# Adjacency: one-hots of two tiles in one DVE operation, alternating with single adds; relation nodes: two relations in each matmul

## The chip, the cores and the metric

The kernel runs on one core of one Trainium2 chip. The metric is the device time of one launch in microseconds (us), as the median of several runs. PE is the matmul engine (PEld its weight loads), DVE the vector engine, ACT the scalar engine, POOL is GpSimd, SP issues most DMAs. Each engine has a sequencer that issues its instructions in program order, waits for semaphores, and does register work in between; rows of a sequencer carry a q behind the engine's name (DVEq).

## The reference, cut to what matters

A stack of four graph layers on 3125 nodes with 48 features and 100000 edges. Two places of it matter here.

```python
# layers 1 and 2: 5 and 10 steps of sums over the edges of the same graph
m = jax.ops.segment_sum(w[:, None] * h[row], col, num_segments=n)
...
msg = f[src] * edge_weight[:, None]
agg = jax.ops.segment_sum(msg, dst, num_segments=n)
...
# layer 3: eight relations, two small layers for each node and relation
h1 = jax.nn.relu(jnp.einsum('ni,rij->nrj', inputs, weight1) + bias1)
h2 = jnp.einsum('nrj,rjo->nro', h1, weight2)
msg = h2[src, rel_type] * norm
agg = jax.ops.segment_sum(msg, dst, num_segments=inputs.shape[0])
return jax.nn.relu(agg + bias2)
```

The sums over edges of layers 1 and 2 are done as products with a dense matrix of the graph, which the stage `adjacency` builds once.

## The kernel before

Nodes lie in 25 blocks (NB) of 128. The edges have been sorted into 1488 tiles of 128 edges, each of one pair of blocks, and four tiles (G) make a group: 372 groups (NG). Stages follow each other with a barrier of all engines between them; the two that are changed are `adjacency` and `relation_nodes`.

**`adjacency`.** For each tile DVE compares a row 0 to 127 with the edge's source and destination numbers, which gives two one-hot matrices of 128 by 128: `turned[..., 2]` for the sources, `hd` for the destinations. PE turns both round (`turn`, for later gathers, stored as OHT) and multiplies them (`products`): once as they are, which counts edges, and once with ACT's widened copy `hs_wide` and its weighted copy `hd_weighted`. DVE then adds each tile's 256 columns to `acc`, at a place that depends on the tile's blocks (`add_up`). When a block of sources is finished, POOL stores its row of ADJ.

Every engine walks through its own list of stages, group by group, in `laps`: a stage with lag 2 works in turn n on group n - 2, six slots hold groups in flight, and a loop over registers covers six groups in a lap, after twelve groups written out. DVE's list (line 876) is: one-hots of the sources of group n (four operations, lines 841 to 843), `rows` for group n - 2, the first add, one-hots of the destinations of group n (four, line 848), and three more adds. `rows` loads four numbers from `row_at` into registers (TENSOR_LOAD, line 853); they hold the places of the four tiles in `acc`. An add waits for the one ahead of it (`s_acc`, line 869), as both may write the same place; the first add of a group also waits for the group's products (`s_sums`).

ACT's list in a turn: widen the sources, weight the destinations, copy the turned matrices of the group before. PE's list: turn, then products.

**`relation_nodes`.** x is turned round to `xT` (48 features by 3200 nodes). Then for each of the eight relations: seven matmuls of at most 512 nodes give the hidden layer (`hidden`, line 2105), ACT adds the bias and cuts at zero (line 2090), 25 matmuls of 128 nodes give h2 with 48 columns each (line 2116), and DVE copies them out of PSUM (line 2126). PE does the hidden layer of relation r + 1 ahead of the products of relation r. When all eight are there, one DMA stores H2 (line 2076), and the stage `relation_pass` gathers rows from it.

Of the kernel before, what the change touches and what calls it, by code (L numbers as in the profile page):

```python
# [18 lines left out]
ALU = mybir.AluOpType  # L19
# [700 lines left out]
def adjacency(nc, mem):  # L720
# [4 lines left out]
    with ExitStack() as ctx:  # L725
# [16 lines left out]
        with nc.Block() as block:  # L742
# [86 lines left out]
            def _(dve):  # L829
                v = nc.vector  # L830
                at = {}

                def column(b, j, at):
                    return rec[:, b, j, at - CW:at - CW + 1]

                def sources(n, b, lap):
                    dve.wait_ge(s_rec[b], 16 * lap + 16)
                    if past(lap, 1):
                        dve.wait_ge(s_sums, n - (SLOTS - 1))
                        dve.wait_ge(s_oht[b], 16 * lap)  # L840
                    for j in range(G):
                        last = v.tensor_scalar(turned[:, b, j, 2], mem["iota_bf"][:], column(b, j, SL), None,
                                               ALU.is_equal)
                    last.then_inc(s_hs, 1)

                def destinations(n, b, lap):
                    for j in range(G):
                        last = v.tensor_scalar(hd[:, b, j], mem["iota_bf"][:], column(b, j, DL), None, ALU.is_equal)
                    last.then_inc(s_hot, 1)

                def rows(n, b, lap):

# [8 lines left out]
                def add_up(j):  # L861

                    def stage(n, b, lap):
# [4 lines left out]
                        if j > 0 or past(n, 1):  # L868
# [119 lines left out]
def past(n, count):  # L988

    return not isinstance(n, int) or n >= count  # L990
# [1063 lines left out]

def relation_nodes(nc, mem, io):

    with ExitStack() as ctx:
        room = Room(nc, ctx, "q_")
        xT = room.sb("xT", [H, NB * P])
        h1T = room.sb("h1T", [H, 2, NB * P])  # L2060
        h2 = room.sb("h2", [P, NB, RELS * H])
        w1 = room.sb("w1", [H, RELS, H])
        w2 = room.sb("w2", [H, RELS, H])
        b1 = room.sb("b1", [H, 1])
        s_w, s_turned, s_copied, s_h1, s_h1c, s_h2, s_h2c, s_out = (
            room.sem(n) for n in ("s_w", "s_turned", "s_copied", "s_h1", "s_h1c", "s_h2", "s_h2c", "s_out"))
        banks = [room.ps(f"bank{b}", [P, 512]) for b in range(2)]
        h2p = [room.ps(f"h2p{b}", [P, 3, 512]) for b in range(2)]
        with nc.Block() as block:
            @block.sync  # L2070
            def _(sp):
                sp.dma_start(w1[:], io["L3_gnn_weight1"].rearrange("r i j -> i r j")).then_inc(s_w, 16)
                sp.dma_start(w2[:], io["L3_gnn_weight2"].rearrange("r i j -> i r j")).then_inc(s_w, 16)
                sp.dma_start(b1[:], io["L3_gnn_bias1"].rearrange("(p o) -> p o", o=1)).then_inc(s_w, 16)
                sp.wait_ge(s_h2c, RELS)
                sp.dma_start(mem["H2"].rearrange("(c p) w -> p c w", p=P), h2[:]).then_inc(s_out, 16)
                sp.wait_ge(s_out, 16)

            @block.scalar
            def _(act):  # L2080
                copy_turned(nc, act, xT, H, banks, s_turned, s_copied)
                act.wait_ge(s_w, 48)
                for r in range(RELS):
                    if r >= 2:
                        act.wait_ge(s_h2, r - 1)
                    for q in range(QUADS):
                        n = min(4, NB - 4 * q) * P
                        m = r * QUADS + q
                        act.wait_ge(s_h1, m + 1)
                        nc.scalar.activation(h1T[:, r % 2, 4 * q * P:4 * q * P + n], banks[m % 2][0:H, 0:n],  # L2090
                                             ACT.Relu, bias=b1[:, 0:1]).then_inc(s_h1c, 1)

            @block.tensor
            def _(pe):
                turn_nodes(nc, pe, mem["x"], H, banks, s_turned, s_copied, mem["ident"][:])
                pe.wait_ge(s_copied, QUADS)
                pe.wait_ge(s_w, 48)

                def hidden(r):
                    for q in range(QUADS):  # L2100
                        n = min(4, NB - 4 * q) * P
                        m = r * QUADS + q
                        if m >= 2:
                            pe.wait_ge(s_h1c, m - 1)
                        nc.tensor.matmul(banks[m % 2][0:H, 0:n], w1[:, r], xT[:, 4 * q * P:4 * q * P + n],
                                         start=True, stop=True).then_inc(s_h1, 1)

                hidden(0)
                for r in range(RELS):
                    if r + 1 < RELS:  # L2110
                        hidden(r + 1)
                    pe.wait_ge(s_h1c, (r + 1) * QUADS)
                    if r >= 2:
                        pe.wait_ge(s_h2c, r - 1)
                    for c in range(NB):
                        last = nc.tensor.matmul(h2p[r % 2][:, c // SPB, (c % SPB) * H:(c % SPB + 1) * H],
                                                h1T[:, r % 2, c * P:(c + 1) * P], w2[:, r], start=True, stop=True)
                    last.then_inc(s_h2, 1)

            @block.vector  # L2120
            def _(dve):
                for r in range(RELS):
                    dve.wait_ge(s_h2, r + 1)
                    for c in range(3):
                        n = min(SPB, NB - c * SPB)
                        last = nc.vector.tensor_copy(h2[:, c * SPB:c * SPB + n, r * H:(r + 1) * H],
                                                     h2p[r % 2][:, c, 0:n * H].rearrange("p (c w) -> p c w", w=H))
                    last.then_inc(s_h2c, 1)


def relation_pass(nc, mem):
# [160 lines left out]
```

## Time and profile before

| | us |
|---|---|
| median of 3 runs | 10251.57 |
| lowest and highest | 10250.43, 10257.3 |
| the profiled execution | 10251.39 |
| its span, first to last instruction | 10249.6 |

Over the span PE is busy 71%, DVE 59%, ACT 37%, POOL 46%. The page's chain of work that ended last is traced back only through the last stage, so it says nothing of the two stages here; they are read from windows and timelines. The profile's busy times count an instruction from its start to the end of its result, so two that follow each other closely overlap: the distance from start to start is what an operation costs in a row of independent ones. Idle time is given in brackets with what ended it; "issue" is time in which the engine waited for nothing that the profile shows.

### The profile page before, as it was taken

How to read it: one execution, taken by the hardware profiler on the slowest of the kernel's cores; microseconds unless marked ns; L12 is line 12 of the kernel's file. 1: busy time of each engine (PE TensorE's matmuls, PEld its weight loads, DVE VectorE, ACT ScalarE, POOL GpSimd, SP SyncE). 2: the span in 40 equal slices, each digit the busy share in tenths (PEclk: the TensorE clock that was granted, in tenths of full speed). 3: DMA queues.
4: the chain of work that ended last, by engine and by line, in shares of the span. 5: the costliest groups of instructions: out<-in, count | busy, mean ns of one | idle time of the engine just before them, and what ended most of it. 6: DMA issues, size and time to landing. Idle time of an engine off the chain costs nothing. (4 is left out here: it accounts for less than half of the span.)

```text
span 10249.6 us, 319174 instructions
## 1 busy us (share of the span) xinstructions
PE 7281.1 (71%) x106850; PEld 5832.8 (57%) x106851; DVE 6047.0 (59%) x19984; ACT 3752.5 (37%) x13000; POOL 4708.0 (46%) x6246
## 2 busy tenths in 40 slices
PE   2888856667657849976994997699488788832332
PEld 1555535555547749966993996699334344432332
DVE  6555558888867779977996998799510000011112
ACT  3222217777743326744772675477100000100000
POOL 0777760000016625533551553355275677256665
PEclk9999998887879979988996998899699999755555
DMA  8222215555439949956992995699488999311112
GB/s 324 60 63 61 62 46 175 183 181 182 132 106 312 310 135 259 262 139 178 262 263 58 260 263 154 165 262 262 138 320 316 351 364 364 130 34 18 18 18 18
DMA packets 1832085, 1846.79 MB, mean 180 GB/s; under 512 B 1450037, under 2 KB 1467989, under 8 KB 1786741
## 3 DMA queue, kind: packets, MB, share of 16 engines
q1 hardware_dynamic: 1717890, 1668.62, 53.0%
q0 software_dynamic: 112016, 153.10, 5.8%
q10 hardware_dynamic: 2016, 22.94, 0.6%
q8 instruction: 97, 1.59, 0.1%
q14 instruction: 66, 0.54, 0.0%
HBM read 1481.79 MB, written 360.62 MB: 180 GB/s over the span
## 5 line engine op out<-in xcount | busy, mean ns | idle before, releaser
L1639 POOL TENSOR_TENSOR s_rest<-s_msg 128x196 f32<-128x196 f32 x1488 | 762.5, 512 | 1912.5 <-ACT s_msg L1621 1861.1
L1231 PE MATMUL s_gotd<-m_table_d,s_hot 128*128 x17856 | 1364.6, 205 | 207.4 <-DMA s_hot<-OHT 195.2
L1621 ACT ACTIVATE s_msg<-s_gotd,s_es 128x49 f32<-128x49 f32 x5952 | 1304.5, 303 | 48.4
L1231 PE MATMUL s_gotq<-m_table_s,s_hot 128*128 x17856 | 1280.9, 185 | 11.3 <-issue 11.3
L1231 PEld LDWEIGHTS s_gotd<-m_table_d,s_hot 128*128 128x128 bf16 x17856 | 990.2, 96 | 293.2 <-DMA s_hot<-OHT 196.3
L1901 POOL DMA_INDIRECT REC<-m_sums x800 | 958.0, 1198 | 354.3 <-issue 347.3
L463 POOL DMA_INDIRECT REC<-rec,place x800 | 960.5, 1201 | 260.5 <-issue 225.8
L2164 POOL DMA_INDIRECT l_row<-H,l_rec x816 | 785.5, 963 | 616.0 <-DMA l_rec<-REC 310.8
L1672 DVE TENSOR_REDUCE s_tops<-s_mt 128x512 f32 (+1 forms) x1488 | 1013.7, 681 | 6.7 <-PE s_mt L1582 6.4
L1934 PE MATMUL p_acc<-p_row,p_feats 128*64 128x512 f32 (+1 forms) x4032 | 900.6, 570 | 160.7 <-DMA p_row<-ADJ 157.8
L1231 PEld LDWEIGHTS s_gotq<-m_table_s,s_hot 128*128 128x128 bf16 x17856 | 993.2, 97 | 7.4 <-issue 7.4
L1245 PE MATMUL l_sums<-l_msg,l_oh 128*128 128x49 f32 x1632 | 371.8, 380 | 824.2 <-issue 807.9
L871 DVE SCALAR_TENSOR_TENSOR a_acc<-a_acc,m_keep,a_sums 128x256 f32 x1488 | 713.2, 479 | 241.2 <-DVE a_acc L871 122.3
L1245 PEld LDWEIGHTS l_sums<-l_msg,l_oh 128*128 128x128 f32 x1632 | 377.2, 322 | 820.1 <-issue 819.9
L1581 PE MATMUL s_mt<-s_hot,m_apart 128*128 128x128 bf16 x5952 | 823.9, 219 | 6.1 <-issue 4.3
L1582 PE MATMUL s_mt<-m_ident_bf,s_raw 128*128 128x128 bf16 x5952 | 824.3, 219 | 1.2 <-issue 1.2
L1646 POOL TENSOR_TENSOR s_least<-s_rest 128x196 bf16<-128x196 f32 x1488 | 762.9, 513 | 116.7
L1934 PEld LDWEIGHTS p_acc<-p_row,p_feats 128*64 128x64 f32 x4032 | 386.1, 141 | 654.6 <-issue 431.1
L822 PE MATMUL a_sums<-a_hd_weighted,a_hs_wide 128*128 128x128 f32 x2976 | 685.3, 359 | 0.0
L1602 PE MATMUL s_sums<-s_msg,s_hot 128*128 128x49 bf16 x5952 | 619.7, 186 | 47.2 <-issue 39.5
L1602 PE MATMUL s_sums<-s_rest,s_hot 128*128 128x49 bf16 x5952 | 620.9, 186 | 0.0
L1602 PE MATMUL s_sums<-s_least,s_hot 128*128 128x49 bf16 x5952 | 619.1, 184 | 0.1
(423 smaller groups left out, 18556.8 us busy)
## 6 DMA issues: line engine op xcount, KB each, us to landing
s_hot<-OHT SPq DMA_DIRECT2D x1488, 384.0 KB
p_row<-ADJ SPq DMA_DIRECT2D x288, 1600.0 KB
s_rec<-REC SPq DMA_DIRECT2D x1488, 98.0 KB
OHT<-a_turned SPq DMA_DIRECT2D x372, 384.0 KB
g_hot<-OHT SPq DMA_DIRECT2D x372, 384.0 KB
ADJ<-a_acc POOLq DMA_DIRECT2D x25, 3200.0 KB
REC<-fill SPq DMA_DIRECT2D x124, 624.0 KB, 10.3
g_rec<-REC SPq DMA_DIRECT2D x372, 108.0 KB
```

Of the source, the lines that this page charges most:

```text
L463: nc.gpsimd.indirect_dma_start(out=mem["REC"], out_offset=bass.IndirectOffsetOnAxis(ap=place[:, b, j:j + 1], axis=0), in_=rec[:, b, j], in ...
L1231: last = nc.tensor.matmul(out, hot, table[k][:, bass.ds(at, w)], start=(k == 0), stop=(k == 2))
L1581: nc.tensor.matmul(mt[:, j], mem["apart"][:], hot[:, b, j, 1], start=True, stop=False)
L1582: last = nc.tensor.matmul(mt[:, j], upper(raw[:, b % KEPT, j:j + 1]).to_broadcast([P, P]), mem["ident_bf"][:], start=False, stop=True)
L1602: last = nc.tensor.matmul(sums[:, 0:SW], hot[:, b, j, 2], thirds[k], start=(j == 0 and k == 0), stop=(j == G - 1 and k == 2))
L1621: last = nc.scalar.activation(msg[:, b % KEPT, j], gotd[b % KEPT][:, j, SW:2 * SW], ACT.Copy, scale=es[:, b % 2, j:j + 1])
L1639: nc.gpsimd.tensor_tensor(rest[:, b % KEPT].rearrange("p g w -> p (g w)"), msg[:, b % KEPT].rearrange("p g w -> p (g w)"), upper(msg[:, b ...
L1646: nc.gpsimd.tensor_tensor(least[:, b % KEPT].rearrange("p g w -> p (g w)"), rest[:, b % KEPT].rearrange("p g w -> p (g w)"), upper(rest[:, ...
L1672: v.tensor_reduce(tops[:, bass.ds(n, 1)], mt[:].rearrange("p j e -> p (j e)"), X, ALU.max).then_inc(s_top, 1)
L1901: nc.gpsimd.indirect_dma_start(out=mem["REC2"], out_offset=bass.IndirectOffsetOnAxis(ap=places_of[b][:, t:t + 1], axis=0), in_=numbers_of[ ...
L1934: last = nc.tensor.matmul(acc[odd * SIDE:(odd + 1) * SIDE, q, 0:n * P].rearrange("w (c e) -> w c e", e=P), feats[:, s], source.rearrange(" ...
L2164: nc.gpsimd.indirect_dma_start(out=row[:, b, j], out_offset=None, in_=table, in_offset=bass.IndirectOffsetOnAxis(ap=rec[:, b, j, GIDX - NO ...
```

## The change

In `adjacency` one DVE operation (`hots`) makes the one-hots of two tiles, as a tensor_tensor from the f32 row `iota` and the f32 record numbers in place of a tensor_scalar from the bf16 row. The list of DVE's stages is written anew: `rows` comes first, and each of the four operations on pairs of tiles stands ahead of one add.

In `relation_nodes` two relations are put side by side: the weights of the hidden layer give 96 output rows in one matmul, and the second weights stand as a 96 by 96 matrix with two blocks on its diagonal, zero elsewhere (a POOL memset, then two DMAs into the blocks). The products go into six PSUM tiles of five nodes' blocks by 96 columns, with a semaphore for each, and H2 is stored in four pieces, one for each pair of relations.

```diff
-                def sources(n, b, lap):
-                    dve.wait_ge(s_rec[b], 16 * lap + 16)
...
-                    for j in range(G):
-                        last = v.tensor_scalar(turned[:, b, j, 2], mem["iota_bf"][:], column(b, j, SL), None,
-                                               ALU.is_equal)
-                    last.then_inc(s_hs, 1)
-
-                def destinations(n, b, lap):
-                    for j in range(G):
-                        last = v.tensor_scalar(hd[:, b, j], mem["iota_bf"][:], column(b, j, DL), None, ALU.is_equal)
-                    last.then_inc(s_hot, 1)
+                def hots(out, b, pair, at):
+                    tiles = slice(2 * pair, 2 * pair + 2)
+                    return v.tensor_tensor(out, mem["iota"][:].unsqueeze(1).to_broadcast([P, 2, P]),
+                                           rec[:, b, tiles, at - CW:at - CW + 1].to_broadcast([P, 2, P]), ALU.is_equal)
+
+                def sources(pair):
+
+                    def stage(n, b, lap):
+                        if pair == 0:
+                            dve.wait_ge(s_rec[b], 16 * lap + 16)
...
+                        last = hots(turned[:, b, 2 * pair:2 * pair + 2, 2], b, pair, SL)
+                        if pair == 1:
+                            last.then_inc(s_hs, 1)
+                    return stage
+
+                def destinations(pair):
+
+                    def stage(n, b, lap):
+                        last = hots(hd[:, b, 2 * pair:2 * pair + 2], b, pair, DL)
+                        if pair == 1:
+                            last.then_inc(s_hot, 1)
+                    return stage
...
-                laps(dve, [(sources, 0), (rows, 2), (add_up(0), 2), (destinations, 0), (add_up(1), 2),
-                               (add_up(2), 2), (add_up(3), 2)], SLOTS)
+                laps(dve, [(rows, 2), (sources(0), 0), (add_up(0), 2), (sources(1), 0), (add_up(1), 2),
+                           (destinations(0), 0), (add_up(2), 2), (destinations(1), 0), (add_up(3), 2)], SLOTS)
...
+    PAIR, FIVE = 2 * H, 5
+    TWOS, PARTS, BANKS = RELS // 2, NB // FIVE, 6
...
+                sp.wait_ge(s_zero, 1)
+                for k in range(2):
+                    sp.dma_start(w2[k * H:(k + 1) * H, :, k * H:(k + 1) * H],
+                                 io["L3_gnn_weight2"].rearrange("(t k) i j -> k i t j", k=2)[k]).then_inc(s_w, 16)
+                for t in range(TWOS):
+                    sp.wait_ge(s_h2c, (t + 1) * PARTS)
+                    sp.dma_start(mem["H2"].rearrange("(c p) w -> p c w", p=P)[:, :, t * PAIR:(t + 1) * PAIR],
+                                 h2[:, :, t * PAIR:(t + 1) * PAIR]).then_inc(s_out, 16)
...
+                        nc.tensor.matmul(banks[m % 2][0:PAIR, 0:n],
+                                         w1[:, 2 * t:2 * t + 2].rearrange("i r j -> i (r j)"),
+                                         xT[:, 4 * q * P:4 * q * P + n], start=True, stop=True).then_inc(s_h1, 1)
...
+                    for c in range(PARTS):
+                        k = t * PARTS + c
+                        if k >= BANKS:
+                            pe.wait_ge(s_h2c, k - BANKS + 1)
+                        for i in range(FIVE):
+                            node = c * FIVE + i
+                            last = nc.tensor.matmul(h2p[k % BANKS][:, i], h1T[:, t % 2, node * P:(node + 1) * P],
+                                                    w2[:, t], start=True, stop=True)
+                        last.then_inc(s_h2, 1)
```

Two places in the engines' order show what moves. The first is one turn of DVE in the adjacency stage before, between two groups of the loop; `a_turned` are the sources, `a_hd` the destinations, `a_acc` an add, ISA the wait ahead of it.

```order
L842 TENSOR_SCALAR a_turned<-m_iota_bf,a_rec 128x128 x4
L853 TENSOR_LOAD m_row_at
L866 REGISTER_ALU x2
L871 ISA
L871 SCALAR_TENSOR_TENSOR a_acc<-a_acc,m_keep,a_sums 128x2x128
L848 TENSOR_SCALAR a_hd<-m_iota_bf,a_rec 128x128 x4
L871 ISA
L871 SCALAR_TENSOR_TENSOR a_acc<-a_acc,m_keep,a_sums 128x2x128
L871 ISA
L871 SCALAR_TENSOR_TENSOR a_acc<-a_acc,m_keep,a_sums 128x2x128
L871 ISA
L871 SCALAR_TENSOR_TENSOR a_acc<-a_acc,m_keep,a_sums 128x2x128
```

The same turn of DVE after the change, from the load to the last add.

```order
L861 TENSOR_LOAD m_row_at
L835 TENSOR_TENSOR a_turned<-m_iota,a_rec 128x2x128
L874 REGISTER_ALU x2
L879 ISA
L879 SCALAR_TENSOR_TENSOR a_acc<-a_acc,m_keep,a_sums 128x2x128
L835 TENSOR_TENSOR a_turned<-m_iota,a_rec 128x2x128
L879 ISA
L879 SCALAR_TENSOR_TENSOR a_acc<-a_acc,m_keep,a_sums 128x2x128
L835 TENSOR_TENSOR a_hd<-m_iota,a_rec 128x256
L879 ISA
L879 SCALAR_TENSOR_TENSOR a_acc<-a_acc,m_keep,a_sums 128x2x128
L835 TENSOR_TENSOR a_hd<-m_iota,a_rec 128x256
```

The last add follows this piece. The one-hots have moved between the adds, the load has moved from behind the sources' one-hots to ahead of their first operation, and the destinations' last operation now stands just ahead of the last add.

The second place is PE in the relation nodes, first the last rows of the stage before; `q_h2p` are the products of the second layer, `q_bank` is the hidden layer.

```order
L2116 MATMUL q_h2p<-q_w,q_h1T 128x48 x25
L2105 MATMUL q_bank<-q_xT,q_w 48x512 x6
L2105 MATMUL q_bank<-q_xT,q_w 48x128
L2116 MATMUL q_h2p<-q_w,q_h1T 128x48 x25
L2105 MATMUL q_bank<-q_xT,q_w 48x512 x6
L2105 MATMUL q_bank<-q_xT,q_w 48x128
L2116 MATMUL q_h2p<-q_w,q_h1T 128x48 x50
```

The same last rows of PE in the stage after the change.

```order
L2141 MATMUL q_h2p<-q_w,q_h1T 128x96 x25
L2126 MATMUL q_bank<-q_xT,q_w 96x512 x6
L2126 MATMUL q_bank<-q_xT,q_w 96x128
L2141 MATMUL q_h2p<-q_w,q_h1T 128x96 x25
L2126 MATMUL q_bank<-q_xT,q_w 96x512 x6
L2126 MATMUL q_bank<-q_xT,q_w 96x128
L2141 MATMUL q_h2p<-q_w,q_h1T 128x96 x50
```

The sequence is the same, but there are four rounds in place of eight, with 96 output rows in the hidden layer and 96 columns in the second. On SP the one DMA of H2 at the stage's end has become four, each behind the copies of its pair of relations.

## Rows read from the trace of the kernel before

**Rows 1.** Windows, the two stages: length, busy us of each engine (instructions), clock, DMA, GB/s.

```profile
1536.00:2975.00 1439.00, 985.17 (x7440) 814.74 (x7440) 1181.60 (x4466) 1038.99 (x2233) 29.20 (x31) 0.82 0.49 164
8831.00:9023.20 192.20, 174.34 (x537) 106.98 (x537) 12.30 (x24) 38.27 (x63) 0.00 (x0) 0.52 0.08 27
```

**Rows 2.** Timeline of DVE, adjacency: start, duration, line, operation, count, [idle before it].

```profile
2013.27 0.48 DVE L871 SCALAR_TENSOR_TENSOR a_acc<-a_acc,m_keep,a_sums 128x256 f32 x1 [0.23 <-issue]
2013.67 0.74 DVE L848 TENSOR_SCALAR a_hd<-m_iota_bf,a_rec 128x128 bf16<-128x128 bf16 x4
2014.32 0.48 DVE L871 SCALAR_TENSOR_TENSOR a_acc<-a_acc,m_keep,a_sums 128x256 f32 x1
2014.96 0.48 DVE L871 SCALAR_TENSOR_TENSOR a_acc<-a_acc,m_keep,a_sums 128x256 f32 x1 [0.17 <-DVE a_acc L871]
2015.61 0.48 DVE L871 SCALAR_TENSOR_TENSOR a_acc<-a_acc,m_keep,a_sums 128x256 f32 x1 [0.17 <-DVE a_acc L871]
...
2016.91 0.48 DVE L871 SCALAR_TENSOR_TENSOR a_acc<-a_acc,m_keep,a_sums 128x256 f32 x1 [0.17 <-issue]
...
2021.19 0.48 DVE L871 SCALAR_TENSOR_TENSOR a_acc<-a_acc,m_keep,a_sums 128x256 f32 x1 [0.81 <-PE a_sums L822]
```

**Rows 3.** Line 853, DVE's sequencer: duration ns min/median/max, first and last start.

```profile
L853 DVEq FUSED_REGOPS  x1: 65/65/65, 2015.9 to 2015.9; - x1
...
L853 DVEq TENSOR_LOAD <-m_row_at x1: 982/982/982, 2019.6 to 2019.6; - x1
```

**Rows 4.** The same line in the last quarter of the stage, 101 loads.

```profile
L853 DVEq TENSOR_LOAD <-m_row_at x101: 340/343/972, 2595.2 to 2969.2; - x101
```

**Rows 5.** Windows, the relation nodes without their start and end.

```profile
8844.00:9006.00 162.00, 161.75 (x497) 102.16 (x497) 10.76 (x21) 30.86 (x51) 0.00 (x0) 0.50 0.00 0
```

**Rows 6.** Timeline of the relation nodes, from the last weight transfers to the next stage.

```profile
8832.29 0.46 SPq L2074 DMA_DIRECT2D q_b<-in_L_gnn_bias  x1
...
8836.58 7.32 PE L2105 MATMUL q_bank<-q_xT,q_w 48*48 48x512 f32 x14 [0.39 <-ACT q_xT L1081]
...
8876.73 10.90 PE L2116 MATMUL q_h2p<-q_w,q_h1T 48*128 48x48 f32 x50
...
8887.56 10.90 PE L2105 MATMUL q_bank<-q_xT,q_w 48*48 48x512 f32 x14
...
8898.39 10.90 PE L2116 MATMUL q_h2p<-q_w,q_h1T 48*128 48x48 f32 x50
...
9006.60 1.54 DVE L2126 COPY q_h<-q_h2p 128x480 f32<-128x480 f32 x3 [9.13 <-PE q_h2p L2116]
9008.17 0.40 SPq L2076 DMA_DIRECT2D H<-q_h  x1
...
9023.95 0.50 PEld L1238 LDWEIGHTS l_sums<-m_zeros,m_nothing 1*128 1x128 f32 x2 [17.55 <-issue]
```

**Rows 7.** Two lines with tensor_tensor on DVE: duration ns min/median/max, starts.

```profile
L565 DVE TENSOR_TENSOR ohb<-sblk,m_iota x100: 682/685/686, 265.1 to 1430.6; 125x512 bf16<-125x512 f32 x100
...
L1391 DVE TENSOR_TENSOR g_gated<-g_rec,g_scaled x372: 349/356/709, 3052.7 to 3662.5; 128x192 f32<-128x192 f32 x186
```

**Rows 8.** Timeline of DVE in an attention stage: a tensor_tensor and the operation behind it.

```profile
4005.61 0.35 DVE L1664 TENSOR_TENSOR s_prod<-s_key,s_gotq 128x196 f32<-128x196 f32 x1
4005.88 0.16 DVE L1684 TENSOR_TENSOR s_diff<-s_diff,m_cap 128x4 f32<-128x4 f32 x1
```

**Rows 9.** Timeline of ACT and of PE, adjacency.

```profile
2010.74 1.28 ACT L791 ACTIVATE a_hd_weighted<-a_hd,a_rec 128x128 f32<-128x128 bf16 x4 [0.68 <-DVE a_hd L848]
...
2024.68 0.31 PE L820 MATMUL a_sums<-a_hd,a_turned 128*128 128x128 bf16 x1
2024.79 0.74 PE L822 MATMUL a_sums<-a_hd_weighted,a_hs_wide 128*128 128x128 f32 x2
2025.32 0.31 PE L820 MATMUL a_sums<-a_hd,a_turned 128*128 128x128 bf16 x1
```

**Rows 10.** Line 1464 in an attention stage, at granted clock 0.50: f32 products with 96 columns.

```profile
L1464 PE MATMUL t_qk<-t_w,t_hT x24: 417/417/417, 4640.7 to 4645.6; 48*128 48x96 f32 x24
```

More of the change, by code:

```diff
@@ L2072, in _ @@
                 sp.dma_start(w1[:], io["L3_gnn_weight1"].rearrange("r i j -> i r j")).then_inc(s_w, 16)
[L2073 to L2077, printed above, removed]
+                for k in range(2):
+                    sp.dma_start(b1[k * H:(k + 1) * H], io["L3_gnn_bias1"].rearrange("(p o) -> p o", o=1)
+                                 ).then_inc(s_w, 16)
+                sp.wait_ge(s_zero, 1)
+                for k in range(2):
+                    sp.dma_start(w2[k * H:(k + 1) * H, :, k * H:(k + 1) * H],
[4 more added lines that the diff above has]
+                                 h2[:, :, t * PAIR:(t + 1) * PAIR]).then_inc(s_out, 16)
+                sp.wait_ge(s_out, 16 * TWOS)
+            @block.gpsimd
+            def _(pool):
+                nc.gpsimd.memset(w2[:], 0.0).then_inc(s_zero, 1)
             @block.scalar
@@ L2081, in _ @@
                 copy_turned(nc, act, xT, H, banks, s_turned, s_copied)
[L2082 to L2085, printed above, removed]
+                act.wait_ge(s_w, 80)
+                for t in range(TWOS):
+                    if t >= 2:
+                        act.wait_ge(s_h2, (t - 1) * PARTS)
                     for q in range(QUADS):
                         n = min(4, NB - 4 * q) * P
-                        m = r * QUADS + q
+                        m = t * QUADS + q
                         act.wait_ge(s_h1, m + 1)
-                        nc.scalar.activation(h1T[:, r % 2, 4 * q * P:4 * q * P + n], banks[m % 2][0:H, 0:n],
+                        nc.scalar.activation(h1T[:, t % 2, 4 * q * P:4 * q * P + n], banks[m % 2][0:PAIR, 0:n],
                                              ACT.Relu, bias=b1[:, 0:1]).then_inc(s_h1c, 1)
@@ L2096, in _, with hidden @@
                 pe.wait_ge(s_copied, QUADS)
-                pe.wait_ge(s_w, 48)
-                def hidden(r):
+                pe.wait_ge(s_w, 80)
+                def hidden(t):
                     for q in range(QUADS):
                         n = min(4, NB - 4 * q) * P
-                        m = r * QUADS + q
+                        m = t * QUADS + q
                         if m >= 2:
                             pe.wait_ge(s_h1c, m - 1)
-                        nc.tensor.matmul(banks[m % 2][0:H, 0:n], w1[:, r], xT[:, 4 * q * P:4 * q * P + n],
-                                         start=True, stop=True).then_inc(s_h1, 1)
+                        nc.tensor.matmul(banks[m % 2][0:PAIR, 0:n],
+                                         w1[:, 2 * t:2 * t + 2].rearrange("i r j -> i (r j)"),
+                                         xT[:, 4 * q * P:4 * q * P + n], start=True, stop=True).then_inc(s_h1, 1)
@@ L2108, in _ @@
                 hidden(0)
[L2109 to L2118, printed above, removed]
+                for t in range(TWOS):
+                    if t + 1 < TWOS:
+                        hidden(t + 1)
+                    pe.wait_ge(s_h1c, (t + 1) * QUADS)
+                    for c in range(PARTS):
[7 more added lines that the diff above has]
+                        last.then_inc(s_h2, 1)
@@ L2120, in _ @@
             @block.vector
             def _(dve):
[L2122 to L2128, printed above, removed]
+                for t in range(TWOS):
+                    for c in range(PARTS):
+                        k = t * PARTS + c
+                        dve.wait_ge(s_h2, k + 1)
+                        nc.vector.tensor_copy(h2[:, c * FIVE:(c + 1) * FIVE, t * PAIR:(t + 1) * PAIR],
+                                              h2p[k % BANKS][:]).then_inc(s_h2c, 1)
```

20 lines of the change are left out of this document (9 added, 11 removed).

## The prediction

> **What bounds the kernel now.** I read the table of windows first, one stretch for each of the two stages that are changed. The adjacency stage takes 1439 us and the relation nodes 192 us; everything else runs the same instructions as before, so I cost only these two [rows 1]. In the adjacency stage no engine is full: DVE is busy 82% (1181.6 of 1439), ACT 72%, PE 68% [rows 1]. The next view is therefore DVE's own timeline, to see what its idle 18% is. One turn of its loop (one group of four tiles) runs from one first add at 2013.27 to the next at 2016.91: 3.64 us [rows 2]. In it an add is followed 0.40 us later by an independent operation (2013.27 to 2013.67), four one-hots take 0.65 (2013.67 to 2014.32), but an add that follows an add starts 0.65 later, not 0.40, after 0.17 us idle "<-DVE a_acc": it waits for the semaphore of the add ahead of it, because both may write the same place of acc. So DVE is the bound here, by its own waits. A third piece is the stretch from the last add, 2015.61, to the next first add, 2016.91: 1.30 us, where 0.40 + 0.65 would be the work. The idle 0.17 there is put down to "issue". The rows of the sequencer say what that is: it issues the four one-hots, works out an address (2015.9), loads four numbers of row_at and does register work before it can issue the add [rows 3]. Proof that this load is on the path: where it takes 982 ns in place of the median 343, the add behind it sits idle 0.81 us in place of 0.17, the same 0.64 more [rows 2 to 4]. Between 2595.2 and 2969.2, where no block of ADJ is stored, 100 groups take 374.0 us, 3.74 each [rows 4]: the plain 3.64 and 0.10 for the jump at the end of each lap of six.
>
> In the relation nodes PE is busy 161.75 of 162 us at a granted clock of 0.50, which is 1.2 GHz [rows 5]. Each relation costs two pieces of 10.90 us, one after the other: 25 products for h2, then seven for the hidden layer [rows 6]. PE alone is the bound; behind it stand a copy of 1.54 us and one store of H2, issued at 9008.17, with the next stage starting at 9023.95: 15.8 us [rows 6].
>
> **The change, adjacency.** Eight operations on 128 elements become four tensor_tensor on 256, from f32 inputs, and each stands between two adds. Price of one: 512 elements of the same comparison with bf16 output take 685 ns [rows 7], 196 elements of an f32 tensor_tensor 0.35 us with the next operation 0.27 us behind it [rows 8]. On the line through both, 256 elements take 0.35 + 60 x (0.685 - 0.35)/316 = 0.41 us, with the next start 0.08 earlier, 0.335. Two old one-hots took 0.65/2 = 0.325 [rows 2], so the work itself is a tie, 4 x 0.335 against 8 x 0.1625: no gain there. The bounds of this price are 0.27 (the start distance of 196 elements) and the 709 ns maximum of another two-input operation [rows 7], taken up below; I take the line, since both its ends are this kind of operation.
>
> The gain is in the order. From add to add there is now 0.40 + 0.335 = 0.735 of work, and the 0.65 that the semaphore asks for lies inside it: the wait is hidden by the one-hots. Three gaps of a turn are of this kind: add0 to add1, to add2, to add3. The fourth, add3 to the next add0, holds the load. The sequencer can issue add3 0.65 after add2 starts (the semaphore). From the issue of a last add to the next first add it needed 1.30 us; it now issues one one-hot there in place of four. The four and a short wait lie between 2015.61 and the address at 2015.9 [rows 2, 3], some 0.06 each, so 0.18 less: 1.12. From add2 to the next add0 that is 0.65 + 1.12 = 1.77, more than the 1.47 of work, so the load still sets this gap, though less of it. A turn is 0.735 + 0.735 + 1.77 = **3.24 us**, and with 0.10 for the lap 3.34 in place of 3.74: 0.40 less. Times 372 groups that is 149 us; the first dozen wait for loads of records and are not in the loop, so I count 360: **144 us**. The stalls where a block of ADJ is stored stay (the load is still on the path).
>
> What is late next? The one-hots of the destinations now end with the turn, not in its middle. Behind the last of them: ACT weights them, 1.28 us [rows 9], PE multiplies, and two turns later add0 needs the product. At 1.2 GHz a pair of products takes 2025.32 - 2024.68 = 0.64 us and a bf16 matmul 0.11 [rows 9], so a group is 4 x 0.64 + 8 x 0.11 = 3.44 us of PE: more than 3.34. At 2.4 GHz it is half, well hidden. The mean granted clock of 0.82 [rows 1] means some 36% of the time at the low level, where a turn costs 3.45: 0.11 x 0.36 x 372 = 15 us given back. ACT's 1039 us are 2.8 per group [rows 1] and still fit. Adjacency: 144 - 15 = **-129 us**.
>
> The Trainium skill, "VectorE: DVE Perf Modes", section on the TRN2 errata, speaks against this part. Its table gives 58 cycles and the elements over the mode's factor: some 94 ns for the old bf16 tensor_scalar at four elements a cycle and 327 ns for the new f32 one at one a cycle. Estimated by that page DVE would have 4 x 327 - 8 x 94 = 0.56 us more work per group, 208 us in all, and the time, with the nodes' gain, would be some 10366; its chance is in rival (4). The trace doesn't bear out the first figure (0.1625 us from start to start [rows 2]), and does the second.
>
> **The change, relation nodes.** Two relations share a product. The hidden layer: four sets of seven instead of eight; each streams the same 512 columns, so a set stays 10.90. The second layer: 4 x 25 products instead of 8 x 25, but each now streams 96 columns, not 48. Is that dearer? The trace has this very shape: 24 records of a 48x128 weight with 96 columns take 4640.7 to 4645.6, 4.9/23 = 0.213 us each [rows 10], against 10.90/50 = 0.218 with 48 columns [rows 6]. The weight load sets the pace, and it stays. So PE loses eight pieces, four relations' worth: 4 x 21.66, the distance from one relation's products at 8876.73 to the next one's at 8898.39 [rows 6], = **86.6 us**. The last copy is one of 480 columns, a third of the 1.54: 0.9 less. The store is cut in four, three under PE's work. The last one moves a quarter of the bytes in as many pieces (3200, of 384 bytes): between a quarter of 15.8 us, 4, and all of it. I take 9, in between, so 6.8 less. Against it: PE waits for two more transfers, behind a GpSimd memset and b1's second copy. The last weight transfer was issued at 8832.29 and PE began at 8836.58 [rows 6]; the new last one goes out some 1.5 us later, so 0 to 2 us, I take 1. PSUM's six smaller banks and 20 copies of some 0.65 us lie under PE. Sum **-93 us**, between -85 and -99.
>
> Total: the profiled execution took 10251.39 us (span 10249.6), as good as the median 10251.57. 10251.4 - 129 - 93 = **10029**.
>
> **The rivals.** (1) The chain through ACT and PE takes over in the adjacency stage: the slack of two turns is used up and the clock stays low more often. At 3.5 us per group throughout the stage gives 0.24 x 372 = 89, the time is 10069, and up to 10110 where ACT adds to it. For: the destinations are late in the turn. Against: at the high clock PE needs half.
> (2) The load hides: DVE then runs at 4 x 0.735 + 0.10 = 3.04, less what the low clock gives back (0.41 x 0.36 x 372 = 55): 260 - 55 + 93 less, 9953. For it: the load now stands ahead of the one-hot, while add3 still runs. Against it: my count of the sequencer.
> (3) PE's clock rises in the relation nodes because the array is fuller. Eight pieces of 10.90 us are left, 87 us; twice the clock would take 43 off, of which I allow 30, since ACT has to empty a bank for every hidden product: 9999. The Trainium skill, "TensorE: Matmul & The Clock Gate", part 1, says that sustained PE work lifts the clock; here 162 us of nothing but PE work had 0.50 [rows 5], and the 96-column rows are at the low pace too [rows 10].
> (4) Slower: the two-input operation on DVE costs what the 709 ns maximum shows [rows 7], from start to start 0.63. A turn is then 4 x 1.03 + 0.10 = 4.22, 0.48 more, 179 us, and with the nodes' 93 the time is 10337. It decides from a turn of 3.99 us, an operation of 0.65 us. Against: that row's minimum is 349, and in its stage GpSimd computes; in this one it only issues stores.
> (5) The adjacency stage doesn't move: 10158.
>
> **How the numbers follow.** Forecast 0.52, (1) 0.17, (2) 0.11, (3) 0.12, (4) 0.04, (5) 0.04. The range, 9955 to 10110, holds the forecast with both its price bounds, (1), (3) and the upper half of (2). About 0.2% (20 us) is what a measurement can tell from no change; every case but (4) is faster by more, so faster 0.95, same 0.01, slower 0.04.
>
> **What would show it.** Right: no "<-DVE a_acc" idle between adds, starts of adds 0.73 to 0.75 apart, some 1.05 around the load; tensor_tensor near 0.41; PE's 25 products still 10.9 us; the next stage some 93 us nearer. Wrong: idle "<-PE a_sums" at the first add (1), no "issue" idle there (2), a clock over 0.5 in the nodes (3), operations near 0.7 (4).

## The result and the profile after

| | us |
|---|---|
| predicted | 10029 (9955 to 10110) |
| median after, 4 runs | 10116.41 (10112.98 to 10118.96) |
| median before, beside it on the same chip, 4 runs | 10254.43 |
| ratio | 0.9864, 95% interval 0.9846 to 0.9881 |
| the profiled execution after, and its span | 10112.98, 10111.1 |

The change gains 138 us, where 222 had been forecast. To see where they are, I read the table of windows first, the two stages again as in [rows 1]. Columns: the stretch, its length, busy time of PE, PEld, DVE, ACT and POOL, PE's granted clock, DMA share, GB/s.

```profile
1536.00:2930.00 1394.00, 944.64 (x7440) 788.12 (x7440) 1149.18 (x2980) 1028.90 (x2233) 29.24 (x31) 0.85 0.50 169
8782.60:8883.00 100.40, 90.64 (x281) 59.43 (x281) 13.14 (x20) 21.05 (x35) 0.41 (x1) 0.52 0.21 51
```

The stage of the relation nodes begins with the first transfer of weights, here before and after:

```profile
8831.15 0.33 SPq L2072 DMA_DIRECT2D q_w<-in_L_gnn_weight  x1
```

```profile
8782.69 0.34 SPq L2082 DMA_DIRECT2D q_w<-in_L_gnn_weight  x1
```

To the first weight load of the next stage (9023.95 [rows 6], 8883.08 after) it takes 100.4 us where it took 192.8: 92.4 less, against 93 forecast. The adjacency stage's last add starts at 2927.0 where it started at 2972.3: 45 less, against 129 forecast. The whole miss is there.

The timeline of DVE, one turn after (start, length, operation, idle time before it in brackets); it answers to [rows 2]:

```profile
2690.44 0.47 DVE L879 SCALAR_TENSOR_TENSOR a_acc<-a_acc,m_keep,a_sums 128x256 f32 x1
2690.84 0.41 DVE L835 TENSOR_TENSOR a_hd<-m_iota,a_rec 128x256 bf16<-128x256 f32 x1
2691.17 0.47 DVE L879 SCALAR_TENSOR_TENSOR a_acc<-a_acc,m_keep,a_sums 128x256 f32 x1
2691.56 0.41 DVE L835 TENSOR_TENSOR a_hd<-m_iota,a_rec 128x256 bf16<-128x256 f32 x1
2691.90 0.47 DVE L879 SCALAR_TENSOR_TENSOR a_acc<-a_acc,m_keep,a_sums 128x256 f32 x1
2692.73 0.42 DVE L835 TENSOR_TENSOR a_turned<-m_iota,a_rec 128x256 bf16<-128x256 f32 x1 [0.36 <-issue]
2693.31 0.48 DVE L879 SCALAR_TENSOR_TENSOR a_acc<-a_acc,m_keep,a_sums 128x256 f32 x1 [0.16 <-issue]
2693.71 0.42 DVE L835 TENSOR_TENSOR a_turned<-m_iota,a_rec 128x256 bf16<-128x256 f32 x1
```

Adds with a one-hot between them start 0.73 apart, and the wait for the add ahead is gone. But from the last add (2691.90) to the next first add (2693.31) there are 1.41 us, no less than the 1.30 of before, though three one-hots have left this gap. It is idle "<-issue", so the next views are the sequencer's rows for the load of row_at (least, median and longest in ns):

```profile
L861 DVEq TENSOR_LOAD <-m_row_at x372: 341/652/1607, 1540.4 to 2923.8; - x186
```

and the line of the adds with some of its waits over the whole stage (us, times), first in the kernel before, then in after:

```profile
L871 DVE SCALAR_TENSOR_TENSOR a_acc<-a_acc,m_keep,a_sums x1488: 470/481/484, 1552.4 to 2972.3; 128x256 f32 x186
...
  DVE a_acc L871: 122.3, 723
```

```profile
L879 DVE SCALAR_TENSOR_TENSOR a_acc<-a_acc,m_keep,a_sums x1488: 468/473/483, 1548.5 to 2927.0; 128x256 f32 x186
...
  DVE a_acc L879: 1.5, 2
  PE a_sums L822: 0.5, 1
```

The load takes 652 ns in the median, where it took 343 [rows 4]. Its mean, without the first four loads of the stage, went from 0.430 to 0.653 us: 0.223 x 368 loads = 82 us. That is the size of the miss, 129 - 45 = 84; the question for the experiments is why the load got slower. Two things changed for it. It now stands right behind an add on DVE. And it now starts beside the store of OHT: the next views are SP's timeline, with the issue of that store, the strip of DMA activity from 2690 to 2694 (40 slices of 0.1 us, busy share in tenths), and the sequencer's row of the one load in this time:

```profile
2690.63 0.35 SPq L773 DMA_DIRECT2D OHT<-a_turned  x1
```

```profile
DMA  0000000000000048999989997335376100000000
```

```profile
L861 DVEq TENSOR_LOAD <-m_row_at x1: 652/652/652, 2691.9 to 2691.9; - x1
```

The store's 384 KB move between 2691.4 and 2692.5; the load starts at 2691.93 in the midst of them and is through at 2692.58. In the kernel before the store went out at 2694.4 behind a load that had started at 2693.6: one was over when the other moved. Its load and its strip, from 2693 to 2697:

```profile
L853 DVEq TENSOR_LOAD <-m_row_at x1: 341/341/341, 2693.6 to 2693.6; - x1
```

```profile
DMA  5200000000000000000000999999989943447710
```

### The profile page after: what moved, and what is told of

Its sections match the earlier page's. It is cut to its first block and busy times, and to the rows that moved or that the text cites. A ratio compares the mean times of both kernels' runs of the same rounds, so it can differ in the third digit from the quotient of the medians.

```text
span 10111.1 us, 317140 instructions
## 1 busy us (share of the span) xinstructions
PE 7157.4 (71%) x106594; PEld 5762.0 (57%) x106595; DVE 6011.7 (59%) x18492; ACT 3729.0 (37%) x12972; POOL 4714.6 (47%) x6247
## 3 DMA queue, kind: packets, MB, share of 16 engines
q8 instruction: 95, 1.56, 0.1%
## 5 line engine op out<-in xcount | busy, mean ns | idle before, releaser
L822 PE MATMUL a_sums<-a_hd_weighted,a_hs_wide 128*128 128x128 f32 x2976 | 660.6, 349 | 0.0
```

## Experiments

Each set of runs had the kernel before beside it on the same chip, and gains are against that median. The kernel before took from 10254 to 10276 us on these chips, so an expectation that is counted from 10254 is compared by its gain and not by its time. The table below gathers what the traces show. Gaps are medians over turns 13 to 371 of the distance from the start of one add to the next, worked out from the start of every add in the trace; the last gap holds the load. The kernels are named by what was changed; their edits follow below.

| kernel | gain, us | ratio, interval | load, median | gaps | turn, median | turn, mean |
|---|---|---|---|---|---|---|
| before | | | 0.343 | 1.05 0.64 0.65 1.30 | 3.65 | 3.83 |
| after | 138 | 0.9864 (0.9846 to 0.9881) | 0.652 | 0.73 0.73 0.73 1.44 | 3.63 | 3.71 |
| after_take_first | 210 | 0.9795 (0.9778 to 0.9811) | 0.344 | 0.73 0.73 0.73 1.12 | 3.30 | 3.52 |
| before_take_first | -51 | 1.0045 (1.0028 to 1.0062) | 0.547 | 1.05 0.64 0.65 1.56 | 3.90 | 3.97 |
| store_after_add3 | 130 | 0.9872 (0.9856 to 0.9889) | 0.344 | 0.73 0.73 0.73 1.12 | 3.30 | 3.70 |
| store_after_add1 | 66 | 0.9946 (0.9929 to 0.9962) | 0.885 | 0.73 0.73 0.73 1.66 | 3.85 | 3.92 |
| order_only | 127 | 0.9879 (0.9863 to 0.9896) | 0.635 | 0.72 0.72 0.72 1.49 | 3.64 | 3.72 |
| merge_only | 115 | 0.9888 (0.9871 to 0.9904) | 0.344 | 1.07 0.64 0.65 1.24 | 3.60 | 3.78 |

From before to after the median turn is hardly shorter, 3.65 and 3.63, but the mean is, by 0.12. The turns by their place in the lap of six, at whose end the loop jumps back, show where the gain sits (medians from the same starts of adds, without turns in which a store of ADJ is issued or that begin up to 14 us behind it):

| place in the lap | 1 | 2 | 3 | 4 (with the jump) | 5 | 6 |
|---|---|---|---|---|---|---|
| before | 3.64 | 3.64 | 3.64 | 4.19 | 3.64 | 3.70 |
| after | 3.60 | 3.57 | 3.62 | 3.85 | 3.46 | 3.71 |
| after_take_first | 3.30 | 3.30 | 3.30 | 3.85 | 3.30 | 3.36 |

In after the gain sits mostly in two turns of six, the one with the jump and the one behind it: over the stage they bring 27 of the 44 us by which all turns together are shorter. At the jump the load starts 0.44 us behind the last add in place of 0.035, which is 1.60 behind the store's issue, and takes 0.349.

### The two halves apart

One kernel has the adjacency stage of after and the relation nodes of before, the other the reverse.

> The adjacency part of the change alone; the relation nodes are the kernel before's. If the trace of after is read rightly (the last add 45 us earlier than before, the relation nodes 92 us shorter), this kernel gains the 45: 10254 - 46 = 10208 us (10200 to 10216). By the prediction's sum it would gain 129 and stand at 10125. The turn should look as in after: adds 0.73 apart, a load of row_at of 0.65 us in the median.

> The relation nodes part alone; the adjacency stage is the kernel before's. By the trace of after and by the prediction (-93): 10254 - 92 = 10162 us (10155 to 10168). If part of the 138 us gained came from something that the two parts do together, this and the other half do not add up to 138.

Measured: 10231.39 and 10184.97 beside 10275.98, so 45 and 91 us less (ratios 0.9952, interval 0.9936 to 0.9969, and 0.9911, 0.9894 to 0.9927). They add up to 136, where after has 138. The halves do not touch each other, and the first one is the one that was mis-sized.

### Moving the store by ACT's list

The store waits for ACT's copy of the turned matrices. Its place in DVE's turn is moved by one edit of ACT's list, made in after and in before; DVE's list is not touched.

```diff
-                laps(act, [(widen, 0), (weighted, 0), (take_turned, 1)], SLOTS)
+                laps(act, [(widen, 0), (take_turned, 1), (weighted, 0)], SLOTS)
```

> After, with ACT's list in another order: it copies the turned matrices of the group before ahead of weighting the destinations, so SP issues the store of OHT about 1.5 us later in DVE's turn, and the load of row_at starts some 3 us behind the last store's issue, as in the kernel before, in place of 1.0 to 1.6. DVE's own list is not touched. Theory A (the load is slowed by the store's transfer): its median goes from 0.65 back to about 0.345 us, its mean from 0.65 to 0.43, and the stage loses 0.22 x 368 = 82 us: 10034 us (10020 to 10055). Theory B (the load is slow because it now stands right behind an add on DVE): median stays 0.65, time stays at 10116 +- 10.

> The same edit of ACT's list in the kernel before, whose DVE list is not touched. There the store is issued about 0.65 us behind the load; with the edit it should be issued some 1.2 us ahead of the next load. Theory A: the load's median rises from 0.343 to about 0.6 us, and the time from 10254 to 10310 to 10360 us. Theory B: load and time stay, 10254 +- 10.

Measured: 10066.39 us, 210 less than before and so, by the two gains, 72 less than after (82 had been expected; in the traces the last add starts 67 us earlier, at 2860.1 in place of 2927.0); and in the kernel before 10326.51, 51 more. The same edit speeds one kernel up and slows the other down, as theory A has it; theory B, that the load is slow behind an add, is out, since in after_take_first it stands behind the same add and takes 0.344. The second gain is a little under what was expected (the load rose to 0.547, not 0.6). The same three views of after_take_first, from 2725 to 2729, with a load on either side of the store:

```profile
2725.35 0.35 SPq L773 DMA_DIRECT2D OHT<-a_turned  x1
```

```profile
DMA  0000000000009999998899334367200000000000
```

```profile
L861 DVEq TENSOR_LOAD <-m_row_at x2: 343/343/343, 2725.0 to 2728.3; - x2
```

The transfer runs from 2726.2 to 2727.3; the loads at 2725.0 and 2728.3 lie outside. In before_take_first the loads of the whole stage are:

```profile
L853 DVEq TENSOR_LOAD <-m_row_at x372: 340/547/1919, 1554.8 to 3030.6; - x186
```

after_take_first beats both kernels. The granted clock of PE is higher in it too, 0.89 where after has 0.84 (1552 to 2850 us), but that is not what shortened the turn: the gap with the load shrank by 0.32, the load itself by 0.31, and the other three gaps stayed at 0.73.

### Moving the store alone

The edit above also makes ACT's copy itself earlier. Here SP alone waits longer, for the fourth or for the second add of the group.

```diff
                     sp.wait_ge(s_turned, n + 1)
+                    sp.wait_ge(s_acc, n * G + 4)
```

> After, with one wait more in SP's list: it issues the store of a group's OHT only when that group's last add is done; in after it goes out some 1.1 us behind the first add, 1.0 to 1.6 us ahead of the load. The lists of DVE, ACT and PE are those of after. The store should now be issued some 0.6 us behind a load and 2.7 us ahead of the next one. Theory A (the transfer beside the load is the whole cause): the load's median is 0.344, the first gap 1.12, the turn 3.30, and the kernel stands with the one in which ACT's order was changed, some 210 us less than before (195 to 220). Rival: what helped there was that ACT copies earlier (PE and ACT themselves run otherwise), and the store's time has nothing to do with it: 138 less, as after.

> The same, but SP waits for the group's second add only: the store then goes out some 0.75 us ahead of the load, which starts earlier in the transfer than in after. Theory A: the few loads of after that started 0.6 to 0.8 us behind a store took 0.78, so the median rises from 0.65 to about 0.78 and the time by 0.13 x 360 = 47 us: 91 us less than before (75 to 115), where after has 138. Rival (only a wait on SP's queue, without effect): 138 less.

Measured: 10134.55 and 10198.97 beside 10264.55, 130 and 66 less. In the quiet turns, away from the stores of ADJ, both do what theory A says: with the store behind the load 0.344, a last gap of 1.12 and a turn of 3.30; with the store 0.8 to 1.0 ahead of it 0.885, a last gap of 1.66. The size of the second was under-estimated: I had gone by a few loads of 0.78. The strip of 2726 to 2730 in store_after_add1 and its load show it: the load starts with the transfer, at 2727.3, and lasts nearly as long:

```profile
DMA  0000000000005979999989747555100000000000
```

```profile
L862 DVEq TENSOR_LOAD <-m_row_at x1: 884/884/884, 2727.3 to 2727.3; - x1
```

SP issues a load of records right behind each store, so that transfer moves along. It does not hold the load of row_at up: in store_after_add3 17 loads lay beside packets of records alone, and took 0.343 in the median, 0.345 at most.

The time of store_after_add3 is not what I expected, and the rival's 138 is nearer to it. The gain of its quiet turns is lost elsewhere: the line of the one-hots has this among its waits (us, times), first in store_after_add3, then in after:

```profile
  DMA a_rec<-REC: 94.5, 25
```

```profile
  DMA a_rec<-REC: 11.7, 12
```

SP's list is in order, so the loads of records queue behind the store that now waits longer. Some 10.5 us behind the issue of each of the 25 stores of ADJ a one-hot sits idle for 3.4 to 4.1 us. In 23 cases it is this wait, with 84.5 of the 94.5 us (the other two of the 25 times lie at the start of the stage); in the remaining two cases the profile names PE's products. Together that is 92 us, which eats the 72 us. The move by ACT's list has no such price (2.2 us of this idle time between 1560 and 2860).

The loads further than 25 us behind the issue of an ADJ store, sorted by the time from the issue of the OHT store to the load's start (worked out from the two lines' rows of the traces named):

| us behind the store | trace | loads | median load, us |
|---|---|---|---|
| 0.8 to 1.0 | store_after_add1 | 174 | 0.885 |
| 1.0 to 1.2 | after | 98 | 0.665 |
| 1.2 to 1.4 | after; before_take_first; store_after_add1 | 37; 99; 34 | 0.645; 0.557; 0.664 |
| 1.4 to 1.6 | after; before_take_first | 57; 76 | 0.500; 0.533 |
| 1.6 to 1.8 | after | 12 | 0.346 |
| 1.8 to 2.0 | before_take_first | 34 | 0.343 |
| 2.8 to 3.0 | before; after_take_first | 140; 91 | 0.342; 0.343 |

### Which half of the adjacency change

Order only keeps the old one-hots, two of them between two adds. Merge only keeps the new one-hots but DVE's old list.

```diff
-                    return v.tensor_tensor(out, mem["iota"][:].unsqueeze(1).to_broadcast([P, 2, P]),
...
+                    for k in range(2):
+                        last = v.tensor_scalar(out[:, k], mem["iota_bf"][:],
...
```

```diff
-                laps(dve, [(rows, 2), (sources(0), 0), (add_up(0), 2), (sources(1), 0), (add_up(1), 2),
-                           (destinations(0), 0), (add_up(2), 2), (destinations(1), 0), (add_up(3), 2)], SLOTS)
+                laps(dve, [(sources(0), 0), (sources(1), 0), (rows, 2), (add_up(0), 2), (destinations(0), 0),
+                           (destinations(1), 0), (add_up(1), 2), (add_up(2), 2), (add_up(3), 2)], SLOTS)
```

> After, with the old one-hots: one bf16 tensor_scalar for each tile, two of them between two adds; the list of DVE's stages and the relation nodes stay as in after. If the gain of the adjacency stage comes from the order, as the prediction has it (0.325 us for two old operations against 0.335 for one new one), it stays but for one dispatch more ahead of the first add, 0.06 x 372 = 22 us: 116 us less than before (105 to 140, where after is 138 less). If the larger operation carries it, only the relation nodes' 92 are left.

> After, with DVE's list in the old order (both pairs of sources, load, first add, both pairs of destinations, three adds one behind the other); one-hots of two tiles in one operation and the relation nodes stay as in after. The waits between adds are back (0.65 each), the store falls behind the load again (load 0.343). By the prediction's reasons the gap from the last add to the first loses two dispatches, 0.12, and the work grows by 0.02: some 37 us less in the stage, so 92 + 37 = 129 us less than before in all (115 to 140). If the sequencer's dispatches cost nothing there: 92 less.

Measured: 10142.9 and 10154.15 beside 10269.61, 127 and 115 less, of which 91 are the relation nodes. So the order is worth 36 us here and the larger operation 24, while both together give 45. Both gains lie in the range that was expected, that of merge_only at its lower end. The order brings the collision with it (0.635), the merging alone does not (0.344). Two old one-hots fill the gap between adds in 0.72, one new one in 0.73: the work is the tie that was forecast. What the larger operation gives is in the last gap, 1.24 against 1.30 with one dispatch for two: 0.07, where 0.12 had been expected.

### Loading fewer times, or less at a time

Since the last gap is set by the load, I tried to load for two groups in every second turn, and to load the four numbers one by one ahead of the add that needs each.

```diff
+                    if b % 2:
+                        return
...
-                        mem["row_at"][0:1, bass.ds(n * G, G)], engines=[dve.engine], min_val=0,
+                        mem["row_at"][0:1, bass.ds(n * G, 2 * G)], engines=[dve.engine], min_val=0,
...
```

> After, with row_at loaded for two groups at once, in every second turn (eight numbers); the turn between has no load between its one-hots and adds. ACT's list is that of after, so the load still meets the store. If the load sets the gap from the last add to the next first one, it falls in every second turn from 1.44 to about 0.75 us: 0.69 x 180 = 124 us less than after, of which PE at its low clock (3.44 us a group) may give back up to 60: 200 to 260 us less than before. If the gap is set by the dispatch of the operations and not by the load, it stays near after, 138 less.

> Both edits: row_at for two groups at once, and ACT's copy of the turned matrices ahead of its weighting. Turns with a load 3.30 us, those without 2.93, 0.09 for the lap: 0.19 x 360 = 67 us less than with the order of ACT alone (which ran 210 less than before), half of the loads beside the stores of ADJ are gone too (18), PE at its low clock gives back some 30: 265 us less than before (230 to 295). If PE and ACT are the bound from 3.3 us on, nothing is gained over 210.

Measured: 10139.57 and 10081.06 beside 10269.61, 130 and 189 less (ratios 0.9876, 0.9859 to 0.9892, and 0.9816, 0.98 to 0.9832): nothing gained over after and 21 us worse than after_take_first. In pairs that is nearer to the rival, that the dispatch sets the gap; but the turns without a load do fall, to 3.01. It is the load of eight that is dear:

```profile
L862 DVEq TENSOR_LOAD <-m_row_at x186: 774/1166/2934, 1542.1 to 2935.1; - x186
```

```profile
L862 DVEq TENSOR_LOAD <-m_row_at x186: 593/599/3006, 1544.7 to 2874.2; - x186
```

Beside the store (first row, pairs) it takes 1166 ns, and a turn with it 4.22 in the median, so that two turns take 3.01 + 4.22 = 7.23, where two of after take 7.25. Without the store (pairs_take_first) it takes 599. Two quiet turns, away from the lap's jump, take 3.01 + 3.55 = 6.56 there, two of after_take_first 2 x 3.30 = 6.60: nothing to gain either. The 21 us lie elsewhere: about half at the lap's jump, where two turns take 7.33 and in after_take_first 7.14 (60 laps, 11 us); the rest is not traced.

```diff
...
-                laps(dve, [(rows, 2), (sources(0), 0), (add_up(0), 2), (sources(1), 0), (add_up(1), 2),
-                           (destinations(0), 0), (add_up(2), 2), (destinations(1), 0), (add_up(3), 2)], SLOTS)
+                laps(dve, [(row(0), 2), (sources(0), 0), (add_up(0), 2), (row(1), 2), (sources(1), 0), (add_up(1), 2),
+                           (row(2), 2), (destinations(0), 0), (add_up(2), 2),
+                           (row(3), 2), (destinations(1), 0), (add_up(3), 2)], SLOTS)
```

> After, with the four numbers of row_at loaded one by one, each ahead of the one-hots and the add that need it, so that each gap between two adds holds a quarter of the load. The load of eight took 0.60 us where none of four took over 0.344 without a transfer beside it: 0.064 for each number, some 0.15 us for one. Theory C (the price goes by the numbers; between two adds the sequencer waits 0.65 us for the semaphore anyway, so a short load is hidden there): the gap from the last add to the first falls from 1.44 to about 1.0, the others stay at 0.73, turn 3.2 in place of 3.6, so 0.35 x 360 = 126 us less than after and up to 35 less beside the stores of ADJ; PE at its low clock gives back up to 60: 235 to 300 us less than before. Rival D (each load costs 0.34 whatever it brings): the first gap stays and the others grow: 100 to 138 us less than before.

> The same with ACT's copy of the turned matrices ahead of its weighting. Theory C: the load of one is 0.15 us without the store beside it, the first gap 0.92, turn 3.1, 0.19 x 360 = 68 us less than with ACT's order alone (210 less than before) and some 35 less beside the stores of ADJ, up to 60 given back by PE at its low clock: 250 to 310 us less than before. Since a short load is hidden in three gaps of four, ACT's order should now matter less than the 72 us that it brought with the load in one place. Rival D: 180 to 210 less.

Measured: 10232.2 and 10255.39 beside 10260.0, only 28 and 5 less (ratios 0.9972, 0.9961 to 0.9983, and 0.9995, 0.9985 to 1.0005). Both theories fall: C because one number costs 0.30 and not 0.15, D because the kernels are slower even than it allowed.

```profile
L862 DVEq TENSOR_LOAD <-m_row_at x1488: 297/304/1627, 1538.6 to 3030.1; - x186
```

Four loads a turn are four chances to meet a transfer: in spread 306 of 1478 loads took over 0.75 us, in after 88 of 368. ACT's order only moves the meeting within the turn: in spread the first of the four loads is the slow one (0.592 in the median), in spread_take_first the second (0.812). The 95th of 100 turns, sorted by length, takes 5.76 in spread and 4.01 in after. From one number to four a load costs little more (0.304 and 0.343), so it should be made once, at a quiet time.

## Why the prediction was right and wrong

**Right in direction and in the relation nodes.** The timeline of PE after, the last copy, the last store and the first matmul of the next stage:

```profile
8788.88 9.02 PE L2126 MATMUL q_bank<-q_xT,q_w 48*96 48x512 f32 x14 [0.71 <-ACT q_xT L1089]
...
8809.15 10.98 PE L2141 MATMUL q_h2p<-q_w,q_h1T 96*128 96x96 f32 x50
8820.06 10.98 PE L2126 MATMUL q_bank<-q_xT,q_w 48*96 48x512 f32 x14
8830.97 10.98 PE L2141 MATMUL q_h2p<-q_w,q_h1T 96*128 96x96 f32 x50
...
8852.79 21.65 PE L2141 MATMUL q_h2p<-q_w,q_h1T 96*128 96x96 f32 x100
```

```profile
8874.47 0.66 DVE L2151 COPY q_h<-q_h2p 128x480 f32<-128x480 f32 x1 [1.48 <-PE q_h2p L2141]
8875.16 0.36 SPq L2092 DMA_DIRECT2D H<-q_h  x1
...
8883.08 0.49 PEld L1246 LDWEIGHTS l_sums<-m_zeros,m_nothing 1*128 1x128 f32 x2 [8.89 <-issue]
```

Pieces are 10.91 apart where they were 10.83 [rows 6], with 96 columns and with 48: the price read from [rows 10] held within 1%. Term by term: PE from its first hidden product to the last copy 85.6 us where it had 170.0 (8836.58 to 9006.60 [rows 6]), 84.4 less (86.6 forecast); the last copy and store 8.6 where they had 17.35, 8.7 less (7.7 forecast; the store itself 7.9, forecast 9); the start 0.8 later (1 forecast). The clock stayed at the low level, 0.52 over the stage, so rival (3) did not happen.

**Right in the adjacency stage.** The new operation takes 0.416 to 0.42 us (0.41 forecast), adds start 0.73 apart (0.735), and the wait "<-DVE a_acc" went from 723 times to 2. The last gap of 1.12, with a load of 343, is what after_take_first and store_after_add3 show (1.12). Rival (1) did not happen: DVE's adds waited for PE's products 0.5 us in all. (The profile puts 22.9 us before one-hots down to PE too, but 51 of these 54 start at most 0.21 behind the end of a load, as a one-hot does that waits for the load alone.) So the time, 10116, lies beside the upper end of rival (1), 10110, for another reason. Nor did (2) happen, the load does not hide; nor (4), the operation is at 0.42, not 0.7; nor (5), the stage moved by 45 us. The 15 us that the low clock was to give back could not show in after, whose turn of 3.63 is longer than the 3.44 of PE at that clock; in after_take_first, with a turn of 3.30, DVE's idle time put down to PE's products is 14.5 us.

**Wrong: two steps of the turn.** First, the sum of the last two gaps, "0.65 + 1.12 = 1.77". It lets the last add go 0.65 behind the third, as the semaphore would. But a one-hot stands between these two as well, and DVE is busy with it: 0.727. The turn is 3 x 0.727 + 1.116 = 3.30, not 3.24, as after_take_first shows: 0.06 to 0.08 x 372, 22 to 29 us.

Second, and much more, the wait for the load in the last gap. The 1.12 is the old gap of 1.30 less three dispatches, so it carries the load over into the new order at its old duration, 343 ns. I read that duration from a kernel in which the load lies between two stores of OHT, and took it for a property of the load. I had even said what lengthens it, a store of ADJ (982 ns [rows 3]), and that such stalls stay; but I did not ask when the other, smaller store goes out in the new turn. The new list puts the destinations' one-hots last, ACT weights them and copies the turned matrices only then, and the store that waits for this copy is mostly issued 1.0 to 1.6 us ahead of the load, where it used to come behind it. The load took 652 ns in the median, and the last gap 1.44. In the mean the load went from 0.430 to 0.653, 82 us. The forecast of 144 less 82 and 22 to 29 leaves 33 to 40 us; 0.12 x 360 = 43 were measured in the mean turn, and 45 in the halves apart.

That so much is left is partly luck. In the turn with the lap's jump the load happens to start late enough to miss the transfer, and that turn and the next bring 27 of the 44 us; the other four turns, which the forecast had 0.40 shorter, are shorter by 0.07 at most.

That the store is the cause is shown twice, by runs that move it and leave DVE's list as it is, in both directions. How the transfer holds the load up is not: it is through about when the store's packets are, yet beside a store of ADJ, with eight times the bytes, it takes 0.9 to 1.0 us, not eight times as long.

## To carry to other kernels

Before you give a wait or a load the duration that it has now, look at what else moves at that moment, and ask whether the new order still keeps the two apart; a DMA whose issue hangs on another engine's work moves with that engine's place in the turn. When a change gains less than its parts say, look for the term that has no new work in it and yet got longer, and move the suspected neighbour rather than the victim. Here one swapped pair in ACT's list brought 72 us on top of the 138 of the whole change.

## What the runs showed of the hardware

A sequencer's load of numbers from SBUF took 0.30 us for one, 0.343 for four and 0.60 for eight (medians) with no transfer beside it. For four it took up to 0.885 in the median beside a store of 384 KB that reads SBUF, and 0.95 beside a store of ADJ (the kernel before). DVE's own operations did not slow: the adds took 468 to 483 ns in after, whatever moved. The Trainium skill, "SBUF — State Buffer", section "Who interferes with whom", says that a DMA does not contend with a compute engine, as it has ports of its own. For DVE's operations the trace agrees, with these 468 to 483 ns; the sequencer's load, which runs ahead of them on the same engine, is slowed all the same.
